# Cross attention on one core: the scores of head 5 move behind the transposes of head 3

## The reference

```
keys   = enc @ Wk            # 718 x 640
scores = q_h @ keys_h.T / sqrt(80)   for each of 8 heads, 100 x 718
probs  = softmax(scores)
hs_h   = probs @ (enc @ Wv_h)
```

## Time and profile before

| what | value |
|---|---|
| median of 3 runs | 1013.64 us (1012.01 to 1024.04) |
| profiled execution, its own time | 1011.86 us |
| its span, first to last instruction | 1010.1 us |
| TensorE busy | 988.2 us, 98% |
| VectorE busy | 677.8 us, 67% |
| ScalarE busy | 489.2 us, 48% |
| GpSimd busy | 343.7 us, 34% |
| granted TensorE clock, mean | 0.994 |

### The profile page before, as it was taken

The page is one execution under the profiler, slowest core; times in us unless marked ns, Lnnn a source line. Parts: engine busy times, 40 slices in busy tenths (PEclk is TensorE's granted clock), DMA queues, the critical chain, the costliest instruction groups (busy, mean ns, idle before and its releaser), DMA issues.

```text
span 1010.1 us, 20729 instructions
## 1 busy us (share of the span) xinstructions
PE 988.2 (98%) x6740; PEld 959.7 (95%) x6740; DVE 677.8 (67%) x1129; ACT 489.2 (48%) x895; POOL 343.7 (34%) x286
## 2 busy tenths in 40 slices
PE   9999899999999999999999999999999999999998
PEld 8998799999999999999999999999999999998997
DVE  6445586767776767676767776777767676766444
ACT  7434455454554545454636363645454545446110
POOL 5212253334242515161615243343333343406000
PEclk9999999999999999999999999999999999999999
DMA  7989967787879777879697878787787877795354
GB/s 264 255 298 272 250 154 198 157 201 168 189 167 195 169 191 171 183 176 186 169 186 184 187 176 190 178 184 187 166 201 162 199 169 190 156 219 160 98 177 148
DMA packets 154169, 190.12 MB, mean 188 GB/s; under 512 B 80928, under 2 KB 108192, under 8 KB 154144
## 3 DMA queue, kind: packets, MB, share of 16 engines
q1 hardware_dynamic: 147456, 177.44, 73.5%
q10 hardware_dynamic: 6688, 12.35, 3.7%
HBM read 81.56 MB, written 19.95 MB: 100 GB/s over the span
## 4 chain that ended last, share of the span: by engine, by line
PE 78%; DMA 7%; SPq 5%; DVE 4%; issue 2%; ACT 2%; POOL 1%; ACTq 0%; DVEq 0%; POOLq 0%
PE psS L750 20%; PE psB L785 19%; PE psB L790 9%; PE psS L725 7%; PE psT L766 6%; PE psS L894 6%; PE psT L812 4%; PE psT L818 2%; SPq L382 2%; DMA kstack<-kT 2%; DMA enc_raw<-in_encN_dram 1%; SPq L379 1%; PE psB L867 1%; PE psB L844 1%; PE psT L819 1%
## 5 line engine op out<-in xcount | busy, mean ns | idle before, releaser
L750 PE MATMUL psS<-encT_keep,Wk_keep 128*128 128x360 f32 x1440 | 253.8, 329 | 0.0
L750 PEld LDWEIGHTS psS<-encT_keep,Wk_keep 128*128 128x128 f32 x1440 | 237.4, 188 | 1.1 <-issue 0.4
L785 PE MATMUL psB<-PT_h,encN_h 120*128 120x400 f32 x576 | 202.3, 351 | 0.0
L785 PE MATMUL psB<-PT_l,encN_h 120*128 120x400 f32 x576 | 198.8, 345 | 0.0
L1133 ACT ACTIVATE probs<-psS,negmax 100x718 f32<-100x718 f32 x128 | 110.2, 861 | 133.5 <-DVE negmax L1524 133.4
L612 POOL TENSOR_TENSOR encT_keep<-encT_raw,encT_keep 128x718 fp32r<-128x718 f32 x45 | 79.7, 1772 | 199.6 <-ACT encT_keep L1162 197.3
L1548 DVE TENSOR_TENSOR kT<-psS,kT 128x718 fp32r<-128x718 f32 x80 | 72.4, 905 | 85.7 <-ACT kT L1157 85.6
L620 POOL TENSOR_TENSOR encN_l<-enc_raw,encN_h 120x768 fp32r<-120x768 f32 x48 | 93.1, 1940 | 90.9 <-ACT encN_h L1169 89.9
L790 PE MATMUL psB<-PT_h,encN_l 120*128 120x400 f32 x576 | 120.3, 344 | 0.8 <-POOL encN_l L620 0.8
L603 POOL TENSOR_TENSOR Mbd<-Mbd,fmask 128x320 fp32r<-128x320 f32 x48 | 46.7, 973 | 218.0 <-DMA Mbd<-m_split 215.4
L1157 ACT ACTIVATE kT<-psS 128x718 fp32r<-128x718 f32 x80 | 61.7, 771 | 115.7 <-PE psS L750 102.5
(11 more groups left out here) (245 smaller groups left out, 1642.2 us busy)
## 6 DMA issues: line engine op xcount, KB each, us to landing
kstack<-kT SPq DMA_DIRECT2D x64, 448.8 KB
kstack<-kT SPq DMA_DIRECT2D x192, 112.2 KB
enc_raw<-in_encN_dram SPq DMA_DIRECT2D x48, 360.0 KB, 5.5
encT_raw<-in_encT_dram SPq DMA_DIRECT2D x45, 359.0 KB, 4.4
kstack<-kT SPq DMA_DIRECT2D x32, 359.0 KB
kstack<-kT SPq DMA_DIRECT2D x32, 269.2 KB
kstack<-kT SPq DMA_DIRECT2D x32, 179.5 KB, 3.2
kstack<-kT SPq DMA_DIRECT2D x64, 89.8 KB, 3.5
```

The costliest lines, as they stand in the source:

```text
L750: mm = pe.matmul(keys_in(f, first)[:, half, 0:HALF], w[:, c, f * 128:(f + 1) * 128], e[:, c, k0:k0 + HALF], start=(j == 0), stop=(j == 3 * ...
L785: pe.matmul(psB[:, 1, 0:RH], eN[0][:, k, cc], PT[p][:, k, rows], start=(k == 0 and p == 0), stop=False)
```

## The change

In `batch` of three engines one step of head 5 is moved. TensorE issues the scores of head 5 after the transposes of head 3. ScalarE takes their exponential after `enc_high(i, 1)`. VectorE takes their maximum after `pt_low(i, 3)`, and normalises them after the maximum of head 6. No instruction is added or removed, and the two other queues are as they were.

```diff
@@ TensorE, batch @@
                     scores(i, 4)
                     if first:
                         query(3, 3)
-                    scores(i, 5)
                     b2_turn(i, 1)
                     if first:
                         query(3, 4)
                     else:
                         context(i - 1, 5)
                     turn(i, 3)
+                    scores(i, 5)
                     b2_xm(i)
@@ ScalarE, batch @@
                     b2_pt_high(i, 1)
-                    expo(i, 5)
...
                     if not last:
                         enc_high(i, 1)
+                    expo(i, 5)
                     xm_high(i)
                     expo(i, 6)
@@ VectorE, batch @@
                     rowmax(i, 4)
                     if first:
                         q_low(3, 3)
-                    rowmax(i, 5)
                     b2_pt_low(i, 1)
                     norm(i, 4)
...
                     pt_low(i, 3)
-                    norm(i, 5)
+                    rowmax(i, 5)
                     xm_add(i)
                     if first:
                         q_low(3, 5)
                     rowmax(i, 6)
+                    norm(i, 5)
                     xm_low(i)
```

## The result

| | before | changed |
|---|---|---|
| median of 6 runs | 1013.11 us | 1030.84 us |
| lowest to highest | 1011.05 to 1024.04 | 1024.61 to 1037.50 |
| profiled execution: span, own time | 1010.1, 1011.86 | 1028.5, 1030.27 |

The ratio is 1.0165, with a 95% interval of 1.0124 to 1.0205. So the changed kernel is slower; that it is by less than 2% is likely but not settled, as the interval reaches over 1.02. The medians differ by 17.7 us, where 10.0 were forecast. The median lies 0.3 us above the upper end of the forecast's range (1030.5), the profiled execution just inside. The profiled executions differ by 18.4 us.

What follows compares the result with a forecast made beforehand. TensorE, busy 98% of the span, was taken as the bound, so only its waits could change. Loop 7.2 plus batch 0's 2.8 gave 10.0 us on 1011.86: 1021.9 us, range 1011 to 1030.5.

Steps and rivals of the forecast that it cites:

- Which wait appears, and its length: TensorE: keys(i + 1, 0) waits for the exponential of head 5; in batch 8 turn comes 0.33 us later.
- E: Start of enc_high(i, 1) on ScalarE, which waits for a load; keys put at E + 1.85, turn(i, 4) at E + 4.82.
- The loop, 7.2 us: 14 batches: load waits of 16.6 us less 0.55 each give 8.9, less 1.7 of hs_add waits: 7.2 us slower.
- E doesn't move: ScalarE: enc_high(i, 1) stays where it was against keys(i, 4), so the loss recurs in each batch.
- named as a sign: Forecast wrong if enc_high(i, 1) starts at another distance from keys(i, 4) than the 15.55 us of batch 8.
- All loads as late as the latest: Upper bound on load landing: 1.1 us a batch, 15.4 + 2.8 = 18.2 us slower, 1030.1 us.
- rival C: Most loads late, as the longer batch shifts them against other memory traffic: 1027 us or more, chance 0.12.
- Rival A: Load there in time, E no later than 545.65 in batch 8, so hidden waits are won: 1007.5 us, chance 0.10.
- Rival B: VectorE: xm_low falls behind the third enc_low, 2.2 us more a batch: 1053 us, slower by over 2%, chance 0.08.
- VectorE and GpSimd: norm(i, 5) ends 0.40 us behind the second enc_low, at E + 3.3; at most 0.1 us cost.
- Batch 0, 2.8 us: Moved matmuls add 0.67 us and keys starts at 127.92, so b2_scores2 comes at 131.34 instead of 128.58: +2.8 us.
- Batch 15, nothing: Last batch has no keys behind it and no load in the way: no cost.

Runs made afterwards that it cites:

- early load: Changed kernel, but SP issues the load of the second third of enc_raw ahead of lift(i, 4) in batches 1 to 14: 1009.8 us, 0.9961 of before.
- late load: Changed kernel, but the second and third third of enc_raw are issued behind load_ga(i + 1) in batches 1 to 14: 1068.6 us, 1.0552 of before.
- the exponential ahead of the load: Changed kernel, but ScalarE takes the exponential of head 5 right behind xm_copy, ahead of enc_high(i, 1): 1017.8 us, 1.0013 of before.

## Why the prediction was right, and where its size was off

*Which wait appears, and its length.* Right. `keys(i + 1, 0)` was put at E + 1.85 and stands at E + 1.74 in each batch. `turn(i, 4)` was put at E + 4.82 and stands there (557.17 - 555.44 + 3.07 = 4.80 in batch 8): the 0.1 too much for the signal is what was too little from keys to `turn`. The early and the late load, 15.6 us less and 39.9 more in the loop, show that E governs it.

*The loop, 7.2 us.* Measured 7.6 in the two traces, 6.6 in the kernel with the change in the loop alone. The sum that took the load's wait from one row and the saved waits from another held. That it came so near has some luck in it. E stood 15.73 us (the change in the loop alone) to 16.36 us (the exponential ahead of the load) behind `keys(i, 4)` in other traces with the load at its old place; by E + 4.80 against the 20.18 us of before, those means alone would make the loop's loss 4.9 to 13.7 us, an estimate.

*E doesn't move.* Right in the mean (15.87 and 15.95). It moves from batch to batch (15.27 to 16.51 us in the changed kernel), and the new order passes on what the old one hid. In the first trace only three of 14 were late enough to cost something, now each 0.1 us counts. In batch 8 itself, which was named as a sign, E went from 15.55 to 15.92 us; `turn(i, 4)` never waited for `hs`, nor `b2_scores2` for `XM`. The spread of the runs says nothing here: it is 13 us for either kernel.

*The bounds and the rivals.* "All loads as late as the latest" was priced too low: it takes 0.64 us off in every batch, but before only three batches waited for `hs_add`. By the same rows it should be 14 x (2.29 - 0.55) - 1.7 + 2.8 = 25.5 us, 1037.3 us; the slowest of the six runs took 1037.50. The median fell where rival C stood (1027 or more, 0.12), though not by its mechanism in the trace at hand, whose loads were hardly later in the mean (15.95 and 15.87 us). Rival A's condition was made by the early load: 1009.8 us where A gave 1007.5. Rival B didn't happen.

*VectorE and GpSimd.* `norm` ended 558.64, 0.40 behind the `enc_low` that ended at 558.24, as I had it; `xm_low` took 0.42 us with GpSimd idle. It started 0.97 us before the third `enc_low` (558.56 and 559.53), so rival B was a margin and stayed one. The Trainium skill (SBUF — State Buffer, "Who interferes with whom") has the instruction that is issued first block the other fully. The trace agrees in the direction, with 1.29 us for a `norm` issued behind an `enc_low` and 0.60 for one that isn't. The `norm` ended 0.40 us behind the `enc_low`, though, which is sooner than its own 0.60, and spans on GpSimd are rough; so a full block isn't shown. What I hadn't seen is that `norm(i, 6)` now runs beside the third `enc_low` and takes 2.19 us. In batch 8 `k_low` starts right behind it (561.67), a little later than it could, and TensorE doesn't wait for that.

*Batch 0, 2.8 us.* The term that was mis-sized: measured 4.2, and 5.6 from `keys(0, 4)` to `keys(1, 4)` with what lies ahead of the moved steps. The moved matmuls add their 0.67 as foreseen (`query(3, 4)` waits 0.95 and not 0.28). But `keys(1, 0)` waited 3.49 us, and the 18 matmuls behind it took longer than anywhere else in this trace:

```profile
130.18 4.74 PE L750 MATMUL psS<-encT_keep,Wk_keep 128*128 128x360 f32 x18 [3.49 <-ACT probs L1133]
```

Windows of the same stretch: us, TensorE busy (instructions), granted clock, DMA share, GB/s.

```profile
126.00:130.00 4.00, 0.69 (x5) 1.00 0.20 52
130.00:135.00 5.00, 4.83 (x21) 0.66 0.00 0
135.00:140.00 5.00, 5.00 (x37) 1.00 0.43 89
```

Behind the wait the clock was granted at 1.2 GHz for a part of five microseconds, and the step from `keys` to `turn` took 4.57 us instead of 2.97. I had priced the wait and not what follows it: +1.6 us. From `turn(0, 3)` to `b2_scores2(0)`, the stretch that the 2.8 were worked out for, it takes 13.2 us in the three kernels with the new order in batch 0 (changed, early load, late load) and 9.0 in the five with the old order on TensorE: 4.2 us, 2.8 + 1.6 within 0.2.

The rest of the 5.6 lies ahead of any moved instruction: `turn(0, 3)` starts 21.88 us behind `keys(0, 4)` and not 20.41. Its beginning is at `turn(0, 2)`, before and changed:

```profile
109.82 0.99 PE L766 MATMUL psT<-ident,probs 100*120 100x100 f32 x6 [2.97 <-DVE PT_l L1537]
```

```profile
111.20 1.23 PE L766 MATMUL psT<-ident,probs 100*120 100x100 f32 x6 [4.23 <-DVE PT_l L1537]
```

It starts 0.46 us later behind `keys(0, 4)` (11.08, not 10.62), and the matmuls behind it stay at half clock for longer (granted 0.50 in 111.20:116.80; 0.54 in 109.80:113.40 before), 1.0 us more up to `turn(0, 3)`. In the experiments `turn(0, 2)` waited from nothing that the trace shows (earlier load in the order of before) to 3.35 us (early load). Since nothing that was moved stands ahead of it on any engine I take this part for chance; but the three kernels with the whole new order in batch 0 have the longest waits, 3.3 to 4.2 us, and no run was made to test it.

*Batch 15, nothing.* In the trace 4.3 us. TensorE waited 4.27 us for `b2_pt_low(15, 1)`, which stood behind a load on ScalarE:

```profile
927.02 1.36 ACT L1212 ACTIVATE Wk_keep<-encT_raw 128x640 fp32r<-128x640 f32 x2 [5.16 <-DMA encT_raw<-in_Wout_dram]
```

Both kernels wait there (before 1.59 us), ahead of the moved steps. In the eight other traces the stretch takes 105.6 to 108.3 us with either order. I take it for chance in this execution; no repeated trace of the changed kernel shows it.

So of 18.4 us between the traces, 7.6 are the loop as forecast and some 4.2 the new order in batch 0. Most of the rest lies where nothing moved stands ahead: 4.3 at the end, 1.5 between `keys(0, 4)` and `turn(0, 3)`, and 0.9 ahead of `keys(0, 4)`. What the traces show of the change is thus 12 us, and the median is 17.7 us higher. Why the median of six runs is as high as the profiled execution, with its unlucky end, stays open. The granted clock of each run is on record and points one way: 0.993 in the fastest of the six (1024.61 us), 0.985 in the slowest (1037.50 us), 0.987 or 0.988 in the other four, against 0.994 in the profiled execution of before. Runs in which more waits were long enough for the clock to fall (last section) would look so, but only their traces could show it.

## What to carry to other kernels

When a step is put behind another on an in-order engine, look first at what that other step waits for: a short instruction behind a load inherits the landing time of the load, and with it its spread. Such a move can be right and still lose: here the same order wins 0.45 us a batch once the load is issued one step earlier. And a kernel's hidden waits are to be read from the distance of starts, since overlapping records don't show them as idle.

## What the runs showed of the hardware

The granted clock fell behind some waits of TensorE and not behind others. The late load gives 14 examples; two neighbours, and windows around them (columns as above):

```profile
240.53 3.27 PE L749 MATMUL psS<-encT_keep,Wk_keep 128*128 128x360 f32 x18 [2.53 <-ACT probs L1132]
...
295.81 4.48 PE L749 MATMUL psS<-encT_keep,Wk_keep 128*128 128x360 f32 x17 [2.47 <-ACT probs L1132]
```

```profile
240.00:244.00 4.00, 3.47 (x23) 1.00 0.31 85
295.50:301.00 5.50, 5.19 (x25) 0.69 0.28 77
352.00:358.50 6.50, 6.16 (x22) 0.50 0.22 61
```

A wait of 2.53 us left the matmuls behind it at 2.4 GHz, one of 2.47 us didn't, and in 10 of 14 batches the step from `keys` to `turn` took 4.3 to 5.6 us, not 3.1; in the other four the wait was 2.31 to 2.97 us. The third window is around the longest of them (5.57 us). In the kernel with the change in the loop alone it happened once, behind a wait of 1.93 us (4.61 us), and not behind one of 1.80. With the exponential moved alone it happened behind 1.65 us already, in batch 6. There it cost nothing: `turn(6, 4)` stands 4.73 us behind `keys(7, 0)`, as in the batches in which it waits for `hs_add`:

```profile
454.85 4.76 PE L750 MATMUL psS<-encT_keep,Wk_keep 128*128 128x360 f32 x18 [1.65 <-ACT probs L1133]
```

```profile
455.00:458.00 3.00, 3.00 (x10) 0.50 0.29 82
```

In the loop of the changed kernel, with waits up to 1.47 us, it never happened. So in these traces a wait of TensorE of 1.65 us or more sometimes cost up to 2.5 us beyond its own length, and its length alone doesn't tell when.

A load issued 3.0 us later landed only 1.7 us later. From issue to landing the second third of `enc_raw` took 3.7 to 5.7 us in the loop of the changed kernel, 3.6 to 3.9 issued later, and 6.1 to 7.3 issued earlier. The time to land isn't fixed; what sets it wasn't tested.
